# A four-layer graph network on one core: one setup program ahead of the first edge pass, and the node numbers worked out beside it

## The chip, the cores and the metric

The kernel runs on one NeuronCore of a Trainium2 chip. The metric is the device time of one execution in microseconds (us). Before the change it is 5416.98 us, the median of three runs (5415.43, 5416.98 and 5417.36).

## The reference

Inputs are x (3125 nodes of 256 features), 50,000 edges (`src`, `dst` sorted by `dst`, `edge_weight`) and the weights of four graph layers. Each layer's result is added to x and layer-normalised:

```python
x = _layernorm(x + _L0_gnn_ref(...))   # GCN: 3 layers of h = x @ fc.T + b; f = (h * deg_out**-0.5) @ ch_w;
                                       # segment_sum(f[src] * edge_w, dst) * deg_in**-0.5; relu; then one MLP
x = _layernorm(x + _L1_gnn_ref(...))   # edge conv: relu(theta(x_dst - x_src) + phi(x_src)), segment_max by dst
x = _layernorm(x + _L2_gnn_ref(...))   # graph attention with self loops, 8 heads, softmax by dst
x = _layernorm(x + _L3_gnn_ref(...))   # 3 edge-conv layers, segment_max by SRC, batch norm
```

`deg_out` and `deg_in` are the counts of edges per source and per destination. The fourth layer needs the edges in the order of `src`, so the kernel sorts them itself.

## The kernel before, in words

Edges are padded to 392 tiles (`ET`) of 128, handled as 98 groups (`NG`) of `GT` = 4 tiles; nodes fill 25 tiles (`NT`). The program is a row of stages, each a `Stage` with its own semaphores; every engine ends a stage before the next begins.

**Setup** is six stages, called at L1851 to L1856 and L1392. `constants` (L261) and `edge_columns` (L424) build identity and index rows and turn the edge lists into columns. `histogram` (L524) runs twice, for `dst` and for `src`: a node number is split into a high digit (98 values) and a low digit (32 values); for 14 tiles (`HB`) at a time VectorE makes both one-hots (L521), TensorE multiplies them per tile (L573), ScalarE keeps each tile's counts in `HIST` (L588); 28 such steps, then VectorE sums `HIST` over all tiles (L553) and sums up the start of each node's edges. Start and count go through DRAM (L599, L611) to become per-node columns. Beside the first histogram SyncE loads all weights (L309); beside the second TensorE turns the weights and multiplies the GCN's `GW` and `GB` (L379), and GpSimd scatters a flag to each node's first edge (`mark`, L650). `src_nodes` (L687) turns `HIST` into running positions with 32 scans (L703), works out the source numbers (`node_numbers`, L613) and the two degree factors. `n0` is a `node_products` stage (L887) that writes the first gather table, with the flags of the source nodes scattered beside it.

**An edge pass** (`edge_pass`, L1096) is a software pipeline over the 98 groups, on every engine in the order of its program. For group g: GpSimd gathers 4 x 128 rows of the table (L1146); ScalarE scales them by the edge weight (L1208, in the three GCN passes `e0` to `e2` alone); TensorE turns them into PSUM (`forth`, L1161); VectorE runs a segmented scan along the edges (`scan`, L1191, two instructions); TensorE turns the result back (`hither`, L1170); ScalarE moves it out (L1215); SyncE stores it and prefetches the indices, masks and weights of the group six further on (L1115 to L1132). In one step TensorE does `forth(g+1)` and then `hither(g)`; `hither(g)` waits for `scan(g)`.

Work "beside" a pass is added to that pipeline by `pipelined` (L84): a list of steps in front of the pass's own (early) and a list behind (late), each with a lead in groups. Two kinds matter here.

- `rank_beside` (L735), in `e0`, `e1` and `e2`: the rank of each edge within its source, for 4 tiles at a time (a rank step). Its parts, in the order in which they depend on each other: one-hots on VectorE (L762, L763), `flip` on TensorE (8 transposes, L787 and L788), `take` on ScalarE (L808 to L810), `meet` on TensorE (L796 to L798, 12 products), `places` on VectorE (L769 to L776). There are 98 rank steps, 33 in each pass (the last has 32), one for every third group. `meet` is an early step, in front of `forth` and `hither`; `places` is an early step of the group after it, in front of that group's `scan`.
- `order_beside` (L817), in `e3`: per group 12 `tensor_scalar` one-hots of full rows against one number per partition (L843 to L845).

Passes `e5` to `e7` have nothing beside them (the attention pass stands between `e3` and `e5`). `node_products` stages stand between the passes; `n4`, ahead of `e3`, uses no GpSimd.

Of the kernel before, what the change touches and what calls it, by code (L numbers as in the profile page):

```python
# [20 lines left out]
GT = 4  # L32
# [51 lines left out]
def pipelined(total, unroll, eng, *steps):  # L84

    most = max(lead for _, lead in steps)
    turns = (total - max(most, 3)) // unroll
# [8 lines left out]
    with eng.Fori(0, turns) as i:  # L98
        for j in range(unroll):
            for fn, lead in steps:  # L100
                fn(i * unroll + (j + lead), (j + lead) % unroll, i + (j + lead) // unroll)
    for s in range(turns * unroll, total):
        straight(s)
# [54 lines left out]
def build(nc, a, out):  # L158
    top = ExitStack()
    Stage.used = []  # L160
    with top:
# [7 lines left out]
        def carve(base, *wanted):  # L169
# [38 lines left out]
        HIST, key_hi, key_lo = carve(ARENA[:, NT * RW:NT * 3 * RW], ((ET, LO), F32), ((ET,), F32), ((ET,), F32))  # L208

        oh_hi, oh_lo, = carve(AGW_BASE, ((2, HB, HI), BF16), ((2, HB, LO), BF16))  # L210
        rank_hi, rank_lo, rank_t, rank_tf, rank_tmp, sel, rank = carve(
            AGW_BASE, ((2, RB, HI), BF16), ((2, RB, LO), BF16), ((2, 2, RB * P), BF16), ((2, RB * P), F32),
# [4 lines left out]
        key_tmp, iota_i, SRCF = carve(WORK, ((3, ET), I32), ((ET,), I32), ((ET,), F32))  # L217
# [12 lines left out]
        MW = sb("MW", [P, LAYERS, 2, D])  # L230
        TH1, DF1, W2 = sb("TH1", [P, 2, D]), sb("DF1", [P, 2, D]), sb("W2", [P, 2, D])
        WA = sb("WA", [P, 2, 2 * HEADS])
        TH3, DF3 = sb("TH3", [P, LAYERS, 2, D]), sb("DF3", [P, LAYERS, 2, D])
# [5 lines left out]
        pos = BYSRC[:, :].bitcast(F32)  # L239
        norm_out, norm_in = sb("norm_out", [P, NT]), sb("norm_in", [P, NT])  # L240
# [3 lines left out]
        MV = sb("MV", [P, NT, 2])  # L244
# [12 lines left out]
        flag_dst, flag_src = dram("flag_dst", [EP, 1]), dram("flag_src", [EP, 1])  # L257
        hist_start, hist_count = dram("hist_start", [2, NP]), dram("hist_count", [2, NP])


        def constants():  # L261
            with Stage(nc, "cst") as st:
                zeroed, filled, done = st.sem("zeroed"), st.sem("filled"), st.sem("done")
                copied = st.sem("copied")
                block = st.block()

                @block.gpsimd
                def _(eng):
                    eng.memset(ident[:, :], 0.0).then_inc(zeroed, 1)
                    eng.memset(ones[:, :], 1.0).then_inc(zeroed, 1)  # L270
                    eng.iota(iota_i[:, :], pattern=[[1, ET]], base=0, channel_multiplier=0).then_inc(zeroed, 1)
                    eng.wait_ge(zeroed, 3)
# [5 lines left out]
                    eng.affine_select(out=upto[:, :], in_=ones[:, :], compare_op=ALU.is_ge, fill=0.0,  # L278
                                      base=0, pattern=[[1, P]], channel_multiplier=-1).then_inc(filled, 1)

                @block.vector
                def _(eng):
                    eng.wait_ge(filled, 3)
                    eng.tensor_copy(identb[:, :], ident[:, :]).then_inc(copied, 1)
                    eng.tensor_copy(iota_b[:, :], iota_i[:, 0:P]).then_inc(copied, 1)
                    eng.tensor_copy(iota_h[:, :], iota_i[:, :]).then_inc(copied, 1)


        def weights_beside():


            fc, ch, mlp, th1, ph1, w2, fcb, fcb_wide, prod, AV = carve(
                WORK[:, 5 * ET:WORK.shape[1]], ((LAYERS * 2, D), F32), ((LAYERS * 2, D), F32), ((2, LAYERS * D), F32),
                ((2, D), F32), ((2, D), F32), ((2, D), F32), ((LAYERS * 2,), F32), ((LAYERS * 2, P), F32),
                ((2, 2, D), F32), ((2, D), F32))
            th3, ph3, B1b = carve(AGW_BASE[:, HB * (HI + LO):NT * RW], ((LAYERS * 2, D), F32), ((LAYERS * 2, D), F32), ((D,), F32))

            turns = [(lambda m, k, l=l: mlp[:, m, l * D + k * P:l * D + k * P + P], MW[:, l]) for l in range(LAYERS)]
            turns += [(lambda m, k: th1[:, m, k * P:k * P + P], TH1[:, :, :]),
                      (lambda m, k: ph1[:, m, k * P:k * P + P], DF1[:, :, :]),  # L300
# [54 lines left out]
            def turn_stage(st):  # L355
# [23 lines left out]
                def on_tensor(eng):  # L379
                    eng.wait_ge(weights_chain, 3 + 2 * LAYERS)  # L380
                    b = 0
                    for nat, _ in turns:
                        if b >= 4:
                            eng.wait_ge(weights_moved, b - 3)
# [1501 lines left out]
```

## Time and profile before

| what | us |
|---|---|
| median of three runs | 5416.98 |
| profiled execution, its span (first to last instruction) | 5421.3 |
| PE busy / DVE busy / ACT busy / POOL busy in it | 3436.3 / 3334.7 / 1890.6 / 3323.9 |
| setup, from 0 to the last tile of the first table | 283.0 |
| first gather of `e0`, `e1`, `e2`, `e3` at | 291.6, 876.1, 1458.8, 2096.8 |
| last gather of the same passes at | 784.2, 1367.8, 1951.3, 2590.6 |

The profile is of one execution, a different one from the three timed runs; its own time stands as its span, 4.3 us above the median. PE is TensorE, PEld its weight loads, DVE VectorE, ACT ScalarE, POOL GpSimd, SP SyncE. A busy share over the whole span mixes stages with different limits, so the rows further down are taken stage by stage.

### The profile page before, as it was taken

To read this page: it belongs to the slowest core of one execution; us is meant where nothing else is said; L and a number is where in the kernel's file an instruction comes from. 1 tells how busy PE (TensorE), PEld (TensorE's weight loads), DVE (VectorE), ACT (ScalarE), POOL (GpSimd) and SP (SyncE) were. 2 spreads that over 40 slices of the span, in tenths; PEclk is the share of its full clock that TensorE was granted. 3 is DMA by queue.
4 is the path that set the end of the run, shared out by engine and by line. 5 is a ranking of instruction groups with operands and counts; after the bars stand their busy time and mean duration, and the time that the engine had idled before them with its cause. 6 is when DMAs were issued, how large, how long until landed. Compare 5 with 4: busy or idle time off the path is not lost. (4 is left out here: it accounts for less than half of the span.)

```text
span 5421.3 us, 80197 instructions
## 1 busy us (share of the span) xinstructions
PE 3436.3 (63%) x18554; PEld 2760.3 (51%) x18554; DVE 3334.7 (62%) x6781; ACT 1890.6 (35%) x4275; POOL 3323.9 (61%) x3460
## 2 busy tenths in 40 slices
PE   3577777777787866666646664455556555665552
PEld 3456665666566655444534442355545555455451
DVE  8856655666566657999657775644444444444444
ACT  2256654666366643222223332222212222122221
POOL 1367765777477744777456664277752777357771
PEclk9778778788877778999666776777778777677776
DMA  3078875888488844888369995288853888358881
GB/s 89 16 197 235 235 210 151 239 234 234 128 236 234 235 136 137 234 233 234 110 170 241 248 242 152 65 230 236 237 163 103 236 237 236 96 169 235 236 230 52
DMA packets 965249, 1026.24 MB, mean 189 GB/s; under 512 B 312526, under 2 KB 843784, under 8 KB 965168
## 3 DMA queue, kind: packets, MB, share of 16 engines
q1 hardware_dynamic: 801184, 582.41, 36.8%
q0 software_dynamic: 163984, 442.92, 31.3%
q8 instruction: 30, 0.49, 0.0%
q14 instruction: 51, 0.42, 0.0%
HBM read 573.30 MB, written 449.41 MB: 189 GB/s over the span
## 5 line engine op out<-in xcount | busy, mean ns | idle before, releaser
L1146 POOL DMA_INDIRECT WORK<-table,idxbuf x2744 | 2609.6, 951 | 1319.6 <-issue 763.8
L1191 DVE TENSOR_TENSOR_SCAN WORK<-maskbuf,WORK,e_fm 128x512 f32<-128x512 bf16 x1372 | 1681.1, 1267 | 1293.7 <-PE e_fm L1161 1287.4
L1161 PE MATMUL e_fm<-ident,WORK 128*128 128x128 f32 x5488 | 997.2, 340 | 1044.1 <-DMA WORK<-table,idxbuf 717.5
L1161 PEld LDWEIGHTS e_fm<-ident,WORK 128*128 128x128 f32 x5488 | 790.1, 175 | 1218.8 <-DMA WORK<-table,idxbuf 725.2
L1215 ACT ACTIVATE WORK<-e_em 128x512 f32<-128x512 f32 x1372 | 757.1, 588 | 1607.6 <-PE e_em L1170 1491.3
L1170 PE MATMUL e_em<-ident,WORK 128*128 128x128 f32 x5488 | 995.2, 342 | 109.4 <-DVE WORK L1191 109.3
L1170 PEld LDWEIGHTS e_em<-ident,WORK 128*128 128x128 f32 x5488 | 884.6, 184 | 134.7 <-issue 112.4
L1208 ACT ACTIVATE WORK<-WORK,wbuf 128x256 f32<-128x256 f32 x1176 | 501.0, 496 | 605.2 <-DMA WORK<-table,idxbuf 605.2
L1545 POOL DMA_INDIRECT WORK<-table_attention,idxbuf x392 | 378.2, 965 | 189.5 <-issue 109.2
L1575 PE MATMUL att_o<-WORK 128*128 128x264 f32 x784 | 297.1, 543 | 0.0
L993 PE MATMUL n_t<-ident,WORK 128*128 128x128 f32 x450 | 108.9, 329 | 264.2 <-DVE WORK L966 156.3
L993 PEld LDWEIGHTS n_t<-ident,WORK 128*128 128x128 f32 x450 | 52.2, 156 | 339.0 <-DVE WORK L966 164.3
L1575 PEld LDWEIGHTS att_o<-WORK 128*128 128x128 f32 x784 | 199.5, 267 | 47.9
L521 DVE TENSOR_TENSOR ARENA<-ARENA,iota_b 128x128 bf16<-128x128 bf16 (+5 forms) x308 | 187.2, 665 | 1.4 <-DVEq L758 0.7
L1662 ACT ACTIVATE WORK<-att_o 128x264 f32<-128x264 f32 x392 | 151.1, 389 | 78.2 <-PE att_o L1575 73.4
L1559 PE MATMUL att_a<-ident,ARENA 128*32 128x128 f32 x98 | 33.4, 341 | 220.7 <-ACT ARENA L1649 220.1
L798 PE MATMUL e_ra<-ARENA 98*128 (+1 forms) x784 | 171.2, 302 | 0.0
L1329 PE MATMUL bn_ps<-ARENA,ones 128*128 128x256 f32 x300 | 105.0, 522 | 89.0 <-DVE ARENA L1355 79.0
L1559 PEld LDWEIGHTS att_a<-ident,ARENA 128*32 128x32 f32 x98 | 9.7, 99 | 274.9 <-ACT ARENA L1649 273.5
L798 PEld LDWEIGHTS e_ra<-ARENA 98*128 98x128 f32 x784 | 126.5, 203 | 28.8
L1329 PEld LDWEIGHTS bn_ps<-ARENA,ones 128*128 128x128 f32 x300 | 77.4, 266 | 116.6 <-DVE ARENA L1355 87.2
L844 DVE TENSOR_SCALAR ARENA<-iota_b,ARENA 128x128 bf16<-128x128 bf16 x392 | 133.3, 340 | 0.0
(282 smaller groups left out, 4519.9 us busy)
## 6 DMA issues: line engine op xcount, KB each, us to landing
edge_results<-WORK SPq DMA_DIRECT2D x686, 512.0 KB
edge_results_attention<-WORK SPq DMA_DIRECT2D x98, 544.0 KB
WORK<-table,idxbuf POOLq DMA_INDIRECT x2744
maskbuf<-nst_dst SPq DMA_DIRECT2D x294, 128.0 KB
maskbuf<-low_src SPq DMA_DIRECT2D x294, 128.0 KB, 4.9
ARENA<-dst_row SPq DMA_DIRECT2D x98, 256.0 KB
table<-ARENA SPq DMA_DIRECT2D x35, 640.0 KB, 3.2
maskbuf<-low_dst SPq DMA_DIRECT2D x98, 128.0 KB
```

Of the source, the lines that this page charges most:

```text
L521: return eng.tensor_tensor(dst, key[:, ds(t, n)].unsqueeze(2).broadcast_to([P, n, width]), iota_b[:, 0:width].unsqueeze(1).broadcast_to([P ...
L798: last = eng.matmul(pa[:, n * LO:(n + 1) * LO], rank_tf[0:HI, b, cols], HIST[0:HI, ds((k + first) * RB + n, 1), :].rearrange("p o l -> p ( ...
L993: last = eng.transpose(tp[slot][:, k * P:(k + 1) * P], R[:, slot, k * P:(k + 1) * P], ident[:, :])
L1146: eng.indirect_dma_start(G[:, q * GT + k, 0:D], None, T, bass.IndirectOffsetOnAxis(ap=idxbuf[:, q, k:k + 1], axis=0)).then_inc(got[q].sem, 16)
L1161: last = eng.transpose(fm[:, q % 2, h, k * P:(k + 1) * P], G[:, q * GT + k, h * P:(h + 1) * P], ident[:, :])
L1170: last = eng.transpose(em[:, pair, k, h * P:(h + 1) * P], S[:, q % 2, h, (2 * pair + k) * P:(2 * pair + k + 1) * P], ident[:, :])
L1191: last = eng.tensor_tensor_scan(S[:, q % 2, h, :], maskbuf[:, q, :], fm[:, q % 2, h, :], S[:, 1 - q % 2, h, GT * P - 1:GT * P], op0, op1)
L1208: last = eng.activation(G[:, q * GT + k, 0:D], G[:, q * GT + k, 0:D], ACT.Copy, scale=wbuf[:, q, k:k + 1])
L1215: eng.activation(O[:, q % 2, 2 * pair:2 * pair + 2, 0:D], em[:, pair], ACT.Copy).then_inc(pairs, 1)
L1329: last = eng.matmul(dst, ones[0:n, :], src[0:n, t, :], start=t == 0, stop=t == NT - 1)
L1545: eng.indirect_dma_start(G[:, q * GT + k, :], None, T2, bass.IndirectOffsetOnAxis(ap=idxbuf[:, q, k:k + 1], axis=0)).then_inc(got[q].sem, 16)
L1575: eng.matmul(po[:, k, 0:TW], same[:, q % 2, k, :], G[:, q * GT + k, :], start=True, stop=True).then_inc(made, 1)
```

## The change

- The six setup stages become one program, `setup()`. It counts the source nodes alone, and uses the counts for `norm_out` and the first table. Its one-hots come in pairs of tiles: keys, index row (`iota2`) and result are bf16, with the two tiles of a pair innermost. TensorE reads each tile of a pair with a step of two elements. GpSimd adds up each step's counts in place of VectorE's sum over `HIST`. Starts and counts become columns by a product with a selection matrix instead of a trip through DRAM. The masks by `dst` come from comparing each edge's `dst` with the one before it instead of a scatter. `GW` and `GB` are made between the two halves of the histogram. The first table's 25 tiles are made in the same program.
- Beside `e0`, now written out without a loop (`flat`), `numbers_and_weights_beside` does the rest: the histogram by `dst` in the first 49 groups (per group 16 `tensor_scalar` one-hots against one number per partition, and 8 accumulating products), the numbers of the source and destination nodes, the loads and turns of all weights not needed at first, and in 32 later groups one of the scans of `HIST` each.
- The 98 rank steps move from `e0` to `e2` into `e1` and `e2`: 49 in each, one for every second group, with three buffers. `meet` and `flip` are both late steps now, behind `hither`.
- The scatter of the source flags moves from `n0` to `n4`.

The core of the diff:

```diff
+        def one_hot_pairs(eng, dst, key, t, n, width):
+            shape = [P, n // 2, width, 2]
+            return eng.tensor_tensor(dst, key[:, ds(t, n)].rearrange("p (a b) -> p a b", b=2).unsqueeze(2).broadcast_to(shape),
+                                     iota2[:, 0:width, :].unsqueeze(1).broadcast_to(shape), ALU.is_equal)
...
+                    eng.memset(added[0:HI], 0.0).then_inc(summed, 1)
+                    with eng.Fori(0, steps) as i:
+                        eng.wait_ge(held, i + 3)
+                        eng.wait_ge(summed, i + 1)
+                        eng.tensor_tensor(added[0:HI], added[0:HI], HIST[0:HI, ds(i * HB, HB), :], ALU.add).then_inc(summed, 1)
...
+                                for k in range(HB):
+                                    last = eng.matmul(wide_ps[0:HI, b, k * LO:(k + 1) * LO], oh_hi[:, b, k // 2, :, k % 2],
+                                                      oh_lo[:, b, k // 2, :, k % 2], start=True, stop=True)
...
+                    hots(0, half // 2)
+                    eng.wait_ge(gcn_in, 14 * 16)
+                    for q in range(2 * LAYERS):
+                        eng.tensor_scalar(fcb_wide[:, q, :], ones[:, :], fcb[:, q:q + 1], None, ALU.mult).then_inc(wide, 1)
+                    hots(half // 2 * 2, (steps - half // 2 * 2) // 2)
...
+                    c.link(eng.tensor_reduce(count_src[:, :], added[0:HI].rearrange("p t l -> p l t"), AX.X, ALU.add))
...
+                        for k in range(DB):
+                            t = g * DB + k
+                            eng.tensor_scalar(dhi[:, g % 2, k, :], iota_b[:, 0:HI], dkey_hi[:, t:t + 1], None, ALU.is_equal)
+                            last = eng.tensor_scalar(dlo[:, g % 2, k, :], iota_b[:, 0:LO], dkey_lo[:, t:t + 1], None, ALU.is_equal)
+                        last.then_inc(dhot, 1)
...
-        RANKS = -(-(ET // RB) // LAYERS)
+        RANKS = ET // RB // 2
...
-                        if q % 3 == phase and not (isinstance(g, int) and g // 3 >= steps):
-                            fn(turn * (SETS // 3) + q // 3, q // 3 % 2)
+                        if q % 2 == phase and not (isinstance(g, int) and g // 2 >= steps):
+                            fn(turn * (SETS // 2) + q // 2, q // 2)
...
-                    return [(at(0, meet), 0)], [(at(0, flip), 2)]
+                    return [], [(at(0, meet), 0), (at(0, flip), 1)]
...
-                    return [(at(0, take), 1)], []
+                    return [(at(0, take), 0)], []
...
-            node_products("n0", stage_copy(X), GW[:, 0], out1, None, out2, table=(AGG, T), marks=(first_src, flag_src))
             for l in range(LAYERS):
-                edge_pass(f"e{l}", SRCI, (ALU.mult, ALU.add), nst_dst, True, rank_beside(l))
+                edge_pass(f"e{l}", SRCI, (ALU.mult, ALU.add), nst_dst, True, rank_beside(l) if l else numbers_and_weights_beside)
...
-            node_products("n4", None, DF1, copy_to(AGG), TH1, out2, table=(AGG, T), norm=(add_bias,))
+            node_products("n4", None, DF1, copy_to(AGG), TH1, out2, table=(AGG, T), norm=(add_bias,), marks=(first_src, flag_src))
...
-        constants()
-        edge_columns()
-        load_weights, turn_weights = weights_beside()
-        histogram(0, DSTF, load_weights)
-        histogram(1, SRCF, both_beside(turn_weights, dst_nodes_beside))
-        src_nodes()
+        setup()
```

## Rows read from the trace of the kernel before

**Rows 1.** The page, costliest groups: the gathers of the seven equal edge passes.

```profile
L1146 POOL DMA_INDIRECT WORK<-table,idxbuf x2744 | 2609.6, 951 | 1319.6 <-issue 763.8
```

**Rows 2.** Windows e1, e3, e5: length, busy PE, PEld, DVE, ACT, POOL, clock, DMA, GB/s.

```profile
876.00:1370.00 494.00, 378.83 (x2315) 316.57 (x2315) 308.90 (x610) 303.74 (x677) 373.45 (x392) 0.80 0.83 231
2097.00:2590.00 493.00, 340.35 (x2295) 241.67 (x2294) 483.59 (x1343) 103.49 (x190) 374.19 (x391) 0.97 0.82 230
3512.00:4001.00 489.00, 280.89 (x1543) 250.20 (x1544) 236.19 (x193) 109.81 (x191) 369.62 (x391) 0.73 0.83 233
```

**Rows 3.** Timeline of DVE in the setup: start, us, what.

```profile
20.13 15.82 DVE L521 TENSOR_TENSOR ARENA<-ARENA,iota_b 128x1372 bf16<-128x1372 bf16 x15 [0.35 <-DVE ARENA L512]
...
117.81 57.02 DVE L521 TENSOR_TENSOR ARENA<-ARENA,iota_b 128x1372 bf16<-128x1372 bf16 x56 [0.34 <-DVE ARENA L512]
177.03 21.69 DVE L553 TENSOR_REDUCE count<-ARENA 98x32 f32<-98x12544 f32 x1 [2.20 <-ACT ARENA L588]
...
209.12 29.73 DVE L703 TENSOR_TENSOR_SCAN ARENA<-ones,startv,ARENA 98x392 f32<-98x392 f32 x32 [5.21 <-PEq L155]
...
282.47 0.48 DVE L1086 SCALAR_TENSOR_TENSOR ARENA<-GB,norm_out,WORK 128x256 f32<-128x256 f32 x1 [0.38 <-ACT WORK L1081]
```

**Rows 4.** Timeline, second histogram: one TensorE step, and GpSimd's scatter beside it.

```profile
124.05 1.35 PE L573 MATMUL hist_ps<-ARENA 128*98 128x32 bf16 x14 [0.69 <-DVE ARENA L521]
124.61 1.73 POOL L650 DMA_INDIRECT flag_dst<-ones,first_dst  x1 [0.30 <-issue]
```

**Rows 5.** Timeline of POOL: a memset of the setup, and a scatter in n0.

```profile
4.51 0.52 POOL L445 MEMSET ARENA<- 98x512 f32 x1
...
244.11 0.97 POOL L650 DMA_INDIRECT flag_src<-ones,first_src  x1 [0.30 <-issue]
```

**Rows 6.** Groups by form, 16 to 210 us: the one-hots of high digits.

```profile
L521 DVE TENSOR_TENSOR ARENA<-ARENA,iota_b 128x1372 bf16<-128x1372 bf16 x56 | 88.6, 1583 | 0.7 <-DVE ARENA L512 0.7
```

**Rows 7.** Timeline of PE: the products of one tile in n0.

```profile
256.28 1.03 PE L1000 MATMUL n_m<-GW,WORK 128*128 128x256 f32 x4
```

**Rows 8.** Timeline of DVE: a scalar per partition, in the setup and in e3.

```profile
106.98 1.26 DVE L365 TENSOR_SCALAR WORK<-ones,WORK 128x128 f32<-128x128 f32 x6
...
2304.11 0.29 DVE L843 TENSOR_SCALAR ARENA<-iota_h,ARENA 128x392 bf16<-128x392 f16 x1
2304.33 0.40 DVE L844 TENSOR_SCALAR ARENA<-iota_b,ARENA 128x128 bf16<-128x128 bf16 x1
```

**Rows 9.** Timeline of e1, its start: meet's first product, forth, places, hither, scan.

```profile
887.68 0.31 PE L796 MATMUL e_rb<-ARENA 98*128 98x128 bf16 x1
...
891.25 1.95 PE L1161 MATMUL e_fm<-ident,WORK 128*128 128x128 f32 x8
891.47 0.29 DVE L769 SCALAR_TENSOR_TENSOR ARENA<-e_rb,upto 128x128 bf16<-128x128 f32 x1 [0.25 <-PE e_ra L798]
...
892.99 1.62 PE L1170 MATMUL e_em<-ident,WORK 128*128 128x128 f32 x8
...
893.42 4.94 DVE L1191 TENSOR_TENSOR_SCAN WORK<-maskbuf,WORK,e_fm 128x512 f32<-128x512 bf16 x4 [0.17 <-PE e_fm L1161]
```

**Rows 10.** The same, later: hither, flip's first and last, take's last, meet's first and last.

```profile
896.02 1.09 PE L1170 MATMUL e_em<-ident,WORK 128*128 128x128 f32 x8 [0.52 <-DVE WORK L1191]
...
896.95 0.22 PE L787 MATMUL e_ra<-identb,ARENA 128*98 128x128 bf16 x1
...
898.14 0.23 PE L788 MATMUL e_ra<-identb,ARENA 128*32 128x128 bf16 x1
...
901.35 0.57 ACT L810 ACTIVATE ARENA<-e_ra 98x512 f32<-98x512 bf16 x1
901.98 0.23 PE L796 MATMUL e_rb<-ARENA 98*128 98x128 bf16 x1 [0.42 <-ACT ARENA L810]
...
903.95 0.41 PE L798 MATMUL e_ra<-ARENA 98*128 x2
```

**Rows 11.** Window of n4, columns as in rows 2.

```profile
2016.00:2089.00 73.00, 55.69 (x250) 42.15 (x250) 53.39 (x200) 35.68 (x100) 0.00 (x0) 0.93 0.10 36
```

More of the change, by code:

```diff
@@ L97, in pipelined @@
         straight(s)
[L98 to L101, printed above, removed]
+    if turns:
+        with eng.Fori(0, turns) as i:
+            for j in range(unroll):
+                for fn, lead in steps:
+                    fn(i * unroll + (j + lead), (j + lead) % unroll, i + (j + lead) // unroll)
     for s in range(turns * unroll, total):
@@ new lines, in build, with one_hot @@
+        count_dst, start_dst, small = (v[0:HI] for v in carve(ROWSUMS, ((LO,), F32), ((LO,), F32), ((LO + 2,), F32)))
+        pick, rows_of = sb("pick", [HI, NT]), sb("rows_of", [HI, 4])
+        START, CNT, HAS, LASTE, T1, T2_ = range(6)
+        def one_hot(eng, dst, key, t, n, width):
+            return eng.tensor_tensor(dst, key[:, ds(t, n)].unsqueeze(2).broadcast_to([P, n, width]),
+                                     iota_b[:, 0:width].unsqueeze(1).broadcast_to([P, n, width]), ALU.is_equal)
@@ new lines, in split, with hots @@
+                    def split(key, hi, lo):
+                        c.inc(eng.tensor_scalar(key_tmp[:, 0], key, LO.bit_length() - 1, None, ALU.arith_shift_right))
+                        c.link(eng.tensor_scalar(key_tmp[:, 1], key, LO - 1, None, ALU.bitwise_and))
+                        c.inc(eng.tensor_copy(hi[:, :], key_tmp[:, 0]))
+                        c.link(eng.tensor_copy(lo[:, :], key_tmp[:, 1]))
+                    split(SRCI[:, :], key_hi, key_lo)
+                    def hots(first, turns):
+                        with eng.Fori(0, turns) as i:
+                            for b in range(2):
+                                n = i * 2 + (first + b)
+                                eng.wait_ge(made, n + 1)
+                                one_hot_pairs(eng, oh_hi[:, b], key_hi, n * HB, HB, HI).then_inc(hot_sem, 1)
+                                one_hot_pairs(eng, oh_lo[:, b], key_lo, n * HB, HB, LO).then_inc(hot_sem, 1)
@@ L602, in histogram @@
[L602 to L611 removed]
+                    eng.wait_ge(dst_in, 48)
@@ new lines, in _, with hold @@
+                    eng.activation(rows_f[:, 1], rows_i[:, 1], ACT.Copy).then_inc(cast_dst, 1)
+                    eng.sem_inc(held, 2)
+                    def hold(first, turns):
+                        with eng.Fori(0, turns) as i:
+                            for b in range(2):
+                                n = i * 2 + (first + b)
+                                eng.wait_ge(made, n + 3)
+                                eng.activation(HIST[0:HI, ds(n * HB, HB), :],
+                                               wide_ps[0:HI, b, 0:HB * LO].rearrange("p (k l) -> p k l", l=LO), ACT.Copy).then_inc(held, 1)
@@ L735, in rank_beside @@
+        RANKS = ET // RB // 2
         def rank_beside(layer):
-            first = layer * RANKS
-            steps = min(RANKS, ET // RB - first)
+            first = (layer - 1) * RANKS
+            steps = RANKS
             def beside(st, name):
```

813 lines of the change are left out of this document (425 added, 388 removed).

## The prediction

> **What bounds the kernel now.** I read the page first, then windows, then timelines, stage by stage. The page's largest group is GpSimd's gathers: 2744 of them, 951 ns each, with 764 us of "issue" between them, which is 1.23 us per gather [rows 1]; the table of times gives 491.7 us for the 391 gaps of `e1`, 1.26 each. Four make a group of edges, so GpSimd alone needs 5.0 us per group and 490 us per pass. The windows say the same of passes with very different work beside them: `e1` with rank steps 494 us, `e3` with 12 one-hots per group 493, `e5` with nothing 489 [rows 2]. So work beside a pass is free as long as it fits into 5.0 us per group. The reader should see how near the limit it already is: in `e3` VectorE is busy 484 of 493 us, in `e1` TensorE 379 of 494.
>
> The setup is bound otherwise, by one engine after another, VectorE above all: the first one-hots start at 20.1 us, 28 steps of the second histogram take 57.0, a sum over `HIST` 21.7, the scans of `HIST` 29.7, and the last tile of the first table is done at 283.0 [rows 3]. The profiled execution's span is 5421.3 us; the median of the runs is 4.3 below it. I apply differences to the median, 5417.
>
> **The setup, part by part.** (a) Up to the first one-hot: 20.1 us now [rows 3]. The new order needs `src` alone, and no stage ends in between; the remaining chain is load, cast, transpose, copy, split. I take 9. (b) 28 steps. One pair of one-hots costs 57.0/28 = 2.04 us now, 1.58 of it the high digits at one element per tick [rows 3, 6]. Packed in pairs the bound above is 2.04 (no gain), below 1.02 (half); I take 1.1. TensorE needs 1.35 per step [rows 4]; its operands get a step of two elements, which no row shows, and I leave it at 1.35 (above: twice). ScalarE is below that. New is GpSimd's addition, 448 elements with two reads and one write. The nearest row is a memset of 512 elements, one write, 0.52 us [rows 5]; one to three times that gives 0.46 to 1.4, and I take 1.05. Does it run beside the one-hots? In the second histogram GpSimd's scatters take 1.73 us and come every 2.03, exactly VectorE's step, while the same scatter in `n0` takes 0.97 [rows 4, 5]. They get one opening per step of VectorE's two-input one-hots. So I add up: 1.1 + 1.05 = 2.15 per step, 60 us; if they overlapped, TensorE would set 1.45 and 41 us.
>
> The Trainium skill's page "SBUF — State Buffer" (section "SBUF: two separate sides") says that a VectorE instruction with two SBUF inputs and a GpSimd one that reads SBUF exclude each other for their whole length. By that rule a step is the sum, by plain overlap TensorE's; the stretched scatters agree with the rule, though they don't show VectorE waiting.
>
> (c) Between the halves TensorE makes `GW` and `GB`: 12 products of 128x256 f32 per layer, 1.03 us per four [rows 7], so 9 us for three layers, plus 8 transposes. VectorE runs two steps ahead meanwhile; net 8. (d) The last step through TensorE, ScalarE and GpSimd, and a sum over 448 elements in place of 21.7 us [rows 3]: 4. (e) 25 tiles, each 1.03 of products and some 0.2 of transposes [rows 7]: 30 with filling the pipeline. Sum: 9 + 60 + 8 + 4 + 30 = 111, against 283.0. That is **-172**; with the overlap -190, with unpaired one-hots (2.04 + 1.05 per step) -146.
>
> What goes for nothing: the histogram by `dst`, its sum, the trips through DRAM and the weights' turns leave the path; what replaces the 32 scans lies in `e0`'s second half, about 1 us per group [rows 3] beside 2.45 of the pass's own scan. The scatter of flags moves to `n4`: 25 times 1.27 us is 32, and GpSimd is idle for all of `n4`'s 73 us [rows 11]. SyncE gets 3.4 MB of loads among `e0`'s stores; DMA is at 0.83 in a pass [rows 2] and gathers run groups ahead.
>
> **e0.** Rank steps go, 16 one-hots against a scalar come, per group for 49 groups. Price: six such in the setup stand 0.195 us apart (128 f32), one of 392 elements in `e3` 0.22 [rows 8]. These are 98 and 32 elements in bf16, shorter than both; below I let the length count and get 0.14, above 0.22. I take 0.17: 2.7 us, with 2.35 for the scan pair 5.05 per group, just at GpSimd's 5.0. The node numbers and weight steps add some 10 us of VectorE, most of which the groups in flight (up to six ahead) hide. **+5**; range -4 to +44 (0.22: 5.9 per group). The products wait for the one-hots (TensorE's late step) but `forth` of the next group is already done, so VectorE's order sets the pace, not the wait.
>
> **e1 and e2.** 49 rank steps per pass instead of 33 look harmless by busy time: TensorE's 379 us in `e1` [rows 2] would become some 440 of 494. But `meet` moves behind `hither`, and the chain closes in two groups instead of three. In order: `meet(k)`, at the end of TensorE's step g; `places(k)`, early in VectorE's step g+1 and so in front of `scan(g+1)`; `scan(g+1)`; `hither(g+1)`, which waits for it; `flip(k+1)` behind it; `forth`, `hither` of the next step; `meet(k+1)`. Nothing of it can overlap: each waits for the one before, by a semaphore or by its engine's order. Lengths: from `meet`'s end (`places` starts at 891.47) to `hither`'s start at 896.02, 4.55 us, places and scan [rows 9, 10]. Then at the high clock `hither` 0.93, `flip` 1.36, `forth` and `hither` 0.93 each (8 like products), `meet` 2.38 [rows 10]: 6.53. Together **11.1 us per two groups**, where GpSimd needs 10.0. `take` (three activations of 0.57) fits beside `forth` and `hither`. Before, the same chain had three groups, 15 us.
>
> At the low clock `forth` takes 1.74 and `meet` 3.79 [rows 9]; with `flip` stretched like `meet` the TensorE part is 11.2, the chain 15.7. Which clock will be granted? `e1` has 0.80 now, `e5` 0.73, `e3` with the densest TensorE work 0.97 [rows 2]; a share of 0.80 is 60% of the time at 2.4 GHz and 40% at 1.2. In the new chain TensorE stands idle for 4.55 - 0.93 = 3.6 us in every eleven, longer than any of its waits in the rows of `e1`, and works without a break otherwise. I take 0.83: the TensorE part is 7.6 (one over 0.66/6.53 + 0.34/11.2), the chain **12.2 us**. 49 of them are 598, against 492 from first to last gather: +106 per pass, **+212** for both. Bounds: 11.1 (+52 each) and 13 (+145 each).
>
> **Sum.** 5417 - 172 + 5 + 212 = 5462; I give 5460. The setup's gain pays for the two passes up to a chain of 11.8 us.
>
> **Rivals.**
> *Faster, the clock stays up.* The chain is there, but TensorE is at 0.9 or more in `e1` and `e2`, as in `e3`: 11.3 us, 554 per pass, +124. 5417 - 172 + 5 + 124 = 5374. For it: TensorE has more to do than in any pass but `e3`. Against: `e3`'s work is spread evenly, here it is one block and one hole. It decides below 11.8 us. Chance 0.30.
> *Much faster, no chain.* Something in the order lets `places` or `meet` slip beside other work, and a rank step costs the 0.1 us that it costs GpSimd now (494 against 489 for 33 of them [rows 2]): 5417 - 172 + 5 + 7 = 5257. Chance 0.08.
> *VectorE bounds e0.* At 0.22 per scalar one-hot: +44 instead of +5, 5500. For it: the 392-element form costs hardly more than the 128-element one, so length may not count at all. Chance 0.10.
> *The pairs don't pay.* The one-hots stay at one element per tick. The bf16 one-hots are at that rate now [rows 6]; no row that I read shows a packed one. Then +26: 5488. The Trainium skill's "VectorE: DVE Perf Modes" (section "The perf-mode tier table") gives `tensor_tensor` in bf16 twice the rate; its condition, steps of one in every operand, is what the pairs are for, and today's broadcast key breaks it, which the rows bear out. Chance 0.07.
> The forecast, within 5400 to 5520, has 0.45.
>
> A measurement of this kernel can tell about 0.2%, 11 us, from no change. From these cases: faster 0.39, within 0.2% 0.06, slower 0.55. The range takes in the clock's two ends with the setup's bounds, 5290 to 5560; the likeliest case alone spans 5400 to 5520.
>
> **What would show it.** First gather of `e0` near 120 us instead of 291.6. In `e1` and `e2` GpSimd's gathers no longer 1.25 apart but held by late prefetches; from one `meet` to the next 11 to 12.5 us; VectorE waiting for TensorE's `meet` ahead of `places`, and TensorE for the scan ahead of `hither`. `e0` at 490 to 500 us, `n4` unchanged. GpSimd's additions alternating with the one-hots, about 2.15 us per step. The forecast is wrong if `e1` stays at 5.0 us per group, or if the granted clock there is near 1.

## The result, and the profile after

The changed kernel takes **5613.0 us** (median of four runs, 5610.9 to 5615.7) against 5417.1 for the kernel before: a ratio of 1.0363, interval 1.0348 to 1.0377, so 3.6% slower. The forecast was 5460, its range 5290 to 5560: the side was right, the size was not, and the result lies 53 us outside the range. The profiled execution's span is 5609.2 us, 187.9 more than that of before. The first and last gathers of the passes say where it went:

| stretch, first gather to first gather | before | after | change | forecast |
|---|---|---|---|---|
| start to `e0` | 291.6 | 115.3 | -176.3 | -172 |
| `e0` to `e1` | 584.5 | 597.1 | +12.6 | +5 |
| `e1` to `e2` | 582.7 | 760.1 | +177.4 | +106 |
| `e2` to `e3` (with `n3`, `n4`) | 638.0 | 815.3 | +177.3 | +106 |
| `e3` to the end | 3324.5 | 3321.4 | -3.1 | 0 |

Two terms are off, and they are the same one twice. The page, costliest groups, shows it at a glance (columns: line engine operation out<-in xcount | busy us, mean ns | idle before us <-what ended most of it):

```profile
L1209 POOL DMA_INDIRECT WORK<-table,idxbuf x2744 | 2616.8, 954 | 1625.3 <-issue 763.3
L1233 PE MATMUL e_em<-ident,WORK 128*128 128x128 f32 x5488 | 1045.1, 354 | 395.5 <-DVE WORK L1254 391.3
L830 DVE SCALAR_TENSOR_TENSOR ARENA<-e_rb,upto 128x128 bf16<-128x128 f32 x392 | 90.5, 287 | 624.9 <-PE e_ra L859 624.9
```

The gathers are as long as before and their "issue" time is the same [rows 1]; their whole idle time has grown by 306 us, nearly all of it spent in something other than issue. `hither` (L1233) waits 391 us for the scan, and the first instruction of `places` (L830) waits 625 us for `meet` (L859): the two waits that the forecast named. Windows of `e1` and of `e3` (length, busy PE, PEld, DVE, ACT, POOL, granted clock, DMA share, GB/s), to be held against [rows 2]:

```profile
712.00:1365.00 653.00, 477.34 (x2636) 385.08 (x2637) 331.84 (x800) 325.76 (x711) 374.31 (x392) 0.74 0.62 173
2288.00:2782.00 494.00, 337.28 (x2297) 240.60 (x2296) 485.32 (x1343) 103.33 (x190) 374.89 (x392) 0.98 0.85 230
```

No engine in `e1` is busy for more than 73% of it, and the DMA share has fallen from 0.83 to 0.62: it is waits that set the pace. Here is one turn of the chain, timelines of TensorE and VectorE (start, us, engine line operation [idle before <-what ended it]):

```profile
909.35 0.41 PE L859 MATMUL e_ra<-ARENA 98*128 x2
909.59 1.07 PE L1224 MATMUL e_fm<-ident,WORK 128*128 128x128 f32 x8
914.21 1.97 PE L1233 MATMUL e_em<-ident,WORK 128*128 128x128 f32 x8 [3.54 <-DVE WORK L1254]
915.97 0.31 PE L848 MATMUL e_ra<-identb,ARENA 128*98 128x128 bf16 x1
...
917.91 1.97 PE L1224 MATMUL e_fm<-ident,WORK 128*128 128x128 f32 x8
919.67 1.53 PE L1233 MATMUL e_em<-ident,WORK 128*128 128x128 f32 x8
921.04 0.22 PE L857 MATMUL e_rb<-ARENA 98*128 98x128 bf16 x1
...
923.25 1.07 PE L1224 MATMUL e_fm<-ident,WORK 128*128 128x128 f32 x8
```

```profile
909.79 0.29 DVE L830 SCALAR_TENSOR_TENSOR ARENA<-e_rb,upto 128x128 bf16<-128x128 f32 x1 [6.37 <-PE e_ra L859]
...
911.62 2.45 DVE L1254 TENSOR_TENSOR_SCAN WORK<-maskbuf,WORK,e_fm 128x512 f32<-128x512 bf16 x2
...
923.45 0.29 DVE L830 SCALAR_TENSOR_TENSOR ARENA<-e_rb,upto 128x128 bf16<-128x128 f32 x1 [6.35 <-PE e_ra L859]
```

From `places` to `places` it is 13.66 us, one turn of the chain, and the turns of both passes all but repeat it (13.5 to 13.9). The parts, from start to start: `places` and scan 4.42 (909.79 to 914.21), `hither` 1.76, `flip` 1.94, `forth` 1.76, `hither` 1.37, `meet` with its way to VectorE 2.41. The TensorE part is 9.24 us; the forecast had 7.6. Look at where the long ones stand: `hither`, `flip` and `forth` behind the wait of 3.54 us take what they take at 1.2 GHz (1.97 for eight products, as [rows 9]), and by the time of `meet` the engine is back at 2.4 (0.22 for its first product; 0.23 in [rows 10]). The windows of this turn say the same: the wait, the TensorE part behind it, and the first 5.46 us of that part.

```profile
910.67:914.21 3.54, 0.00 (x0) 0.01 (x1) 3.30 (x8) 0.00 (x0) 2.63 (x4) 0.95 0.69 165
914.21:923.45 9.24, 9.24 (x50) 7.52 (x51) 2.89 (x5) 6.63 (x15) 4.20 (x5) 0.65 0.57 159
914.21:919.67 5.46, 5.46 (x25) 4.40 (x25) 2.88 (x4) 2.85 (x6) 3.99 (x5) 0.50 0.50 147
```

The columns are those of the windows above. The granted clock is still 0.95 while TensorE waits, 0.50 in the 5.46 us behind the wait, and 0.65 over the whole TensorE part (the medians over 89 turns of both passes are the same); the mean of the pass, 0.74, lies between.

The setup, timelines of VectorE, TensorE and GpSimd: the first pair of one-hots, twelve steps in the second half, the sum, the last tile of the first table; then one step of TensorE, and two of GpSimd's additions.

```profile
9.85 2.26 DVE L262 TENSOR_TENSOR WORK<-ARENA 128x1372 bf16<-128x1372 bf16 x4 [0.35 <-DVE ARENA L494]
...
47.80 22.51 DVE L262 TENSOR_TENSOR WORK<-ARENA 128x1372 bf16<-128x1372 bf16 x24 [7.80 <-PE set_wide L424]
...
73.76 0.90 DVE L517 TENSOR_REDUCE count_src<-WORK 98x32 f32<-98x448 f32 x1 [3.05 <-POOL WORK L341]
...
106.30 0.48 DVE L536 SCALAR_TENSOR_TENSOR ARENA<-GB,norm_out,WORK 128x256 f32<-128x256 f32 x1 [0.60 <-ACT WORK L588]
```

```profile
55.41 1.35 PE L424 MATMUL set_wide<-WORK 128*98 128x32 bf16 x14 [0.52 <-DVE WORK L262]
```

```profile
55.86 1.12 POOL L341 TENSOR_TENSOR WORK<-WORK,ARENA 98x448 f32<-98x448 f32 x1 [0.75 <-ACT ARENA L560]
...
72.67 0.98 POOL L341 TENSOR_TENSOR WORK<-WORK,ARENA 98x448 f32<-98x448 f32 x1 [0.89 <-ACT ARENA L560]
```

A step is 22.51/12 = 1.88 us. The first four one-hots, with no addition beside them yet, take 2.26, which is 1.13 for a step's pair (the forecast had 1.1); later VectorE counts as busy all the time and takes 1.88 for the same pair, and each addition starts 0.75 us after the one before it ends. An addition takes 1.12 us beside the one-hots and 0.98 once they are over.

### The profile page after: what moved, and what is told of

Same layout as the page of the kernel before. It is cut to its first block and busy times, and to the rows that moved or that the text cites. A ratio compares the mean times of both kernels' runs of the same rounds, so it can differ in the third digit from the quotient of the medians.

```text
span 5609.2 us, 78920 instructions
## 1 busy us (share of the span) xinstructions
PE 3510.0 (63%) x18564; PEld 2818.3 (50%) x18564; DVE 3331.3 (59%) x7488; ACT 1868.6 (33%) x4237; POOL 3324.5 (59%) x3471
## 5 line engine op out<-in xcount | busy, mean ns | idle before, releaser
L1224 PE MATMUL e_fm<-ident,WORK 128*128 128x128 f32 x5488 | 1024.1, 347 | 1020.6 <-DMA WORK<-table,idxbuf 793.3
L1224 PEld LDWEIGHTS e_fm<-ident,WORK 128*128 128x128 f32 x5488 | 821.6, 180 | 1180.0 <-DMA WORK<-table,idxbuf 775.1
L1233 PE MATMUL e_em<-ident,WORK 128*128 128x128 f32 x5488 | 1045.1, 354 | 395.5 <-DVE WORK L1254 391.3
L1233 PEld LDWEIGHTS e_em<-ident,WORK 128*128 128x128 f32 x5488 | 921.4, 191 | 443.3 <-issue 386.9
L830 DVE SCALAR_TENSOR_TENSOR ARENA<-e_rb,upto 128x128 bf16<-128x128 f32 x392 | 90.5, 287 | 624.9 <-PE e_ra L859 624.9
L1053 PE MATMUL n_t<-ident,WORK 128*128 128x128 f32 x400 | 96.3, 327 | 224.6 <-DVE WORK L1026 159.9
L1060 PE MATMUL n_m<-TURNED,WORK 128*128 128x256 f32 x600 | 177.0, 423 | 0.0
L859 PE MATMUL e_ra<-ARENA 98*128 (+1 forms) x784 | 161.0, 288 | 0.0
L1064 PE MATMUL n_m<-TURNED,WORK 128*128 128x256 f32 x600 | 159.2, 389 | 0.0
```

The lines of the kernel that those rows point to most:

```text
L859: last = eng.matmul(pa[:, n * LO:(n + 1) * LO], rank_tf[0:HI, b, cols], HIST[0:HI, ds((k + first) * RB + n, 1), :].rearrange("p o l -> p ( ...
L1060: last = eng.matmul(mps[:, slot, 0:D], XT[:, slot, k * P:(k + 1) * P], w1[:, k, :], start=k == 0, stop=k == 1)
L1064: last = eng.matmul(mps[:, slot, D:D + n2], XT[:, slot, k * P:(k + 1) * P], w2[:, k, :], start=k == 0, stop=k == 1)
L1224: last = eng.transpose(fm[:, q % 2, h, k * P:(k + 1) * P], G[:, q * GT + k, h * P:(h + 1) * P], ident[:, :])
L1233: last = eng.transpose(em[:, pair, k, h * P:(h + 1) * P], S[:, q % 2, h, (2 * pair + k) * P:(2 * pair + k + 1) * P], ident[:, :])
```

## The experiments

Each run stands against runs of the kernel before on the same chip. Edits are to the changed kernel unless said otherwise.

### places behind the scan

```diff
-                    return [(at(1, places), 0)], [(at(0, one_hots), 3)]
+                    return [], [(at(1, places), 0), (at(0, one_hots), 3)]
```

> The changed kernel with one step moved: VectorE does places behind the scan of its group instead of in front of it, same operations, same counts. Theory of the closed chain (meet, places, scan, hither, flip, forth, hither, meet: 13.66 us per two groups in e1 and e2 of the changed kernel): scan and hither leave the chain, what stays is meet 2.4, places 1.8, flip 1.4 to 1.9, forth and hither 1.9 to 3.5, which is 7.5 to 9.6 and below GpSimd's 10.0. e1 and e2 go back to 492 to 500 us from first to last gather, about 170 us less each with the tail: 5260 to 5285 in all. Rival, 49 rank steps per pass are too much work (TensorE at the clock it is granted, or VectorE): order is no cure, e1 and e2 stay above 600 us, the total above 5500.

5254.6 us (5252.7 to 5260.1), ratio to before 0.971, interval 0.9694 to 0.9726. One step moved past another on one engine is worth 358 us. The window of `e1`, and a turn on TensorE and VectorE:

```profile
713.00:1205.00 492.00, 426.44 (x2677) 345.97 (x2677) 342.83 (x803) 325.30 (x721) 372.43 (x392) 0.83 0.83 231
```

```profile
952.08 1.09 PE L1233 MATMUL e_em<-ident,WORK 128*128 128x128 f32 x8 [0.91 <-DVE WORK L1254]
...
955.64 0.29 DVE L830 SCALAR_TENSOR_TENSOR ARENA<-e_rb,upto 128x128 bf16<-128x128 f32 x1 [1.21 <-PE e_ra L859]
```

`e1` is at 491.4 us with all its 49 rank steps, GpSimd is the bound again, and `hither` waits 0.91 us in place of 3.54. So neither the count of rank steps nor their cost on any engine was at fault. All that differed was that `scan` stood behind `places`, and through it `hither` behind `meet`.

### The hole filled with needless work

```diff
                     def hither(g, q, turn):
+                        if name in ("e1", "e2") and q % 2 == 1:
+                            eng.wait_ge(pairs, g * 2 + 3)
+                            for k in range(24):
+                                eng.transpose(em[:, 0, k % 2, k // 2 % 2 * P:(k // 2 % 2 + 1) * P], ident[:, :], ident[:, :])
                         eng.wait_ge(scanned, g + 3)
```

> The changed kernel with 24 needless TensorE products (128x128 f32, target e_em, overwritten afterwards) ahead of hither's wait in every second group of e1 and e2, where TensorE stands idle for 3.5 us: more work, the same chain. Theory that the hole is what keeps the clock down in the first six us of each block: 24 at 0.116 us are 2.8 us and fit in the hole, hither, flip and forth run at the high rate, the period falls from 13.66 to 4.4 + 3 x 0.93 + 1.36 + 2.4 = 11.0 us, 130 us less per pass, 5350 in all, though TensorE does more. Rival, the clock is low for another reason (too much work, or the level of the chip): the 24 take 5.3 us, 1.8 more than the hole, the period is 15.5 and the total 5790.

5339.8 us (5334.1 to 5345.5), ratio 0.9864, interval 0.9844 to 0.9884: 273 us less than the changed kernel, by adding 2352 products to it.

```profile
715.00:1241.00 526.00, 477.89 (x3776) 406.34 (x3776) 333.59 (x801) 322.62 (x713) 372.34 (x391) 0.98 0.77 215
```

```profile
911.03 2.78 PE L1231 MATMUL e_em<-ident 128*128 128x128 f32 x24
914.66 1.09 PE L1237 MATMUL e_em<-ident,WORK 128*128 128x128 f32 x8 [0.84 <-DVE WORK L1258]
915.59 0.22 PE L848 MATMUL e_ra<-identb,ARENA 128*98 128x128 bf16 x1
...
916.94 1.09 PE L1224 MATMUL e_fm<-ident,WORK 128*128 128x128 f32 x8
```

The clock is at 0.98, `hither` takes 0.93 to the next start where it took 1.76, and the turn is 10.82 us (median of 96). That is the forecast's length at the high clock, 11.1, to within 0.3; the chain was laid out rightly, and the clock was the whole of the error. The Trainium skill's page "TensorE: Matmul & The Clock Gate" (section "HAM oscillation — how this bites in real kernels") describes the like for a loop that waits for a transfer in every turn: each burst of products starts at half clock again. The traces agree: with a wait of 3.54 us in each turn `hither`, `flip` and `forth` run at the low clock, with one of 0.84 none of them does.

### places made longer, take made longer

```diff
-                        eng.wait_ge(passed, k * 6 + 5)
-                        eng.tensor_reduce(rank[:, 1, :], sel[:, :, :], AX.X, ALU.add).then_inc(passed, 1)
-                        eng.wait_ge(passed, k * 6 + 6)
+                        for n in range(4):
+                            eng.wait_ge(passed, k * 9 + (n + 5))
+                            eng.tensor_reduce(rank[:, 1, :], sel[:, :, :], AX.X, ALU.add).then_inc(passed, 1)
+                        eng.wait_ge(passed, k * 9 + 9)
```

> The changed kernel with three more reductions of 128x128 in places, each behind the one before: about 0.37 us each, 1.1 us in all. Chain theory: places lies on the chain, so each of the 98 periods grows by 1.1 us: +110 us, 5720 in all, although VectorE is busy for half of e1 and e2 alone. Rival, something else sets the pace (TensorE's work, GpSimd, a transfer): within 15 us of 5613.

5771.3 us (5767.2 to 5775.4): +158, where 110 was expected; three reductions are 0.96 us, and 98 of those 94.

```profile
712.00:1441.00 729.00, 530.48 (x2632) 421.94 (x2632) 369.22 (x937) 328.37 (x711) 373.73 (x391) 0.61 0.54 155
```

```profile
915.79 0.41 PE L860 MATMUL e_ra<-ARENA 98*128 x2
916.03 1.07 PE L1225 MATMUL e_fm<-ident,WORK 128*128 128x128 f32 x8
921.62 1.97 PE L1234 MATMUL e_em<-ident,WORK 128*128 128x128 f32 x8 [4.52 <-DVE WORK L1255]
...
929.25 0.64 PE L860 MATMUL e_ra<-ARENA 98*128 x2
```

The turn goes from 13.66 to 15.36 us on average (turns of 14.4 and 16.3 alternate). 0.96 of the 1.70 is the work; the rest is that the hole has grown (4.5 us in one turn, 3.7 in the next) and that the low clock lasts longer behind it, in the second turn shown into `meet` (0.64 for two of its products, 0.41 in the turn before). The clock of the pass is 0.61.

For `take` the same was tried with two more activations in front of its three (each waiting for the one before it).

> The changed kernel with two more activations of 98x512 in take, each behind the one before: 1.2 to 1.3 us more on ScalarE in each of 98 rank steps. Chain theory: take ends 1.5 us ahead of meet, beside forth and hither, so it is off the chain: within 15 us of 5613. Rival, any engine's extra work shows because all are coupled: +120 us.

5612.3 us (5609.7 to 5614.9), a turn of 13.66 us: nothing, for 98 times 1.15 us of ScalarE (382.0 us busy in `e1`, where it was 325.8). Together the two runs draw the chain: a microsecond on it costs more than itself, one beside it costs nothing.

### meet back in front

```diff
-                    return [], [(at(0, meet), 0), (at(0, flip), 1)]
+                    return [(at(0, meet), 0)], [(at(0, flip), 1)]
```

> The same kernel as before under this edit, since that run's chip moved about 160 GB/s in the passes in place of 235 and made them wait for transfers. Theory of the chain in two groups: meet 2.4, scan and places 4.4, hither 0.93, flip 1.4, take 1.9: 11.0 at the high clock, up to 13 at the low one; e1 and e2 take 540 to 640 us, the total is 5330 to 5560. Rival, the late meet alone is to blame: 492 to 500 us each and 5255.

5400.0 us (5391.1 to 5404.1), ratio 0.9957, interval 0.9943 to 0.9972; `e1` takes 556.5 us, a turn 11.35 (median). So the late `meet` alone isn't it: put back, the chain closes through `take` (`meet` waits 1.64 us for ScalarE) and is still above the 10 us of two groups.

```profile
916.56 0.23 PE L857 MATMUL e_rb<-ARENA 98*128 98x128 bf16 x1 [1.64 <-ACT ARENA L871]
...
919.31 1.95 PE L1224 MATMUL e_fm<-ident,WORK 128*128 128x128 f32 x8
```

The low clock is here too (0.77 in `e1`): the longest wait of this turn is 1.64 us, and `forth` behind `meet` takes 1.95. So a wait of 3.5 us is not the only thing that brings it.

### The kernel before, with meet late

```diff
-                    return [(at(0, meet), 0)], [(at(0, flip), 2)]
+                    return [], [(at(0, meet), 0), (at(0, flip), 2)]
```

> The same kernel as before under this edit, for the same reason. Chain theory: 13.7 us is below the 15 that three groups give, so nothing changes: within 10 us of the kernel before. Rival, a late meet costs 3.66 us per rank step: +350 us.

5543.4 us (5541.9 to 5545.0), ratio 1.0224, interval 1.0205 to 1.0243. Both expectations missed. I had carried the 13.66 over; but with three groups to a rank step the order of TensorE's program runs through one more `forth` and `hither`, and the wait ahead of `hither` is there as well:

```profile
959.37 1.96 PE L1170 MATMUL e_em<-ident,WORK 128*128 128x128 f32 x8 [3.54 <-DVE WORK L1191]
961.12 0.31 PE L787 MATMUL e_ra<-identb,ARENA 128*98 128x128 bf16 x1
```

A turn is 16.3 us, above the 15.0 of three groups. At the high clock it should be 12.7 (10.8 and the 1.9 of one more `forth` and `hither`). That was then tried, with the same 24 products in every third group of the three passes:

> The same kernel as before under this edit, whose run was on a chip with slower transfers (7.3 us per group whatever the order). Theory: 12.9 us at the high clock, below the 15 of three groups, so the passes go back to 492 to 496 us and the total to 5415 to 5430, though work is added. Rival: 5540 and more.

5432.8 us (5422.4 to 5440.7), ratio 1.0022, interval 1.0010 to 1.0033; the turn is 15.0, GpSimd's, and `e1` has 493.4 us at a clock of 0.93. So in this kernel, too, it is the clock that makes the chain bind. That it is 12.7 us at the high clock is not shown: the run says only that it is below the 15.0 of three groups.

### The setup: unpaired one-hots, and no addition on GpSimd

The first edit puts `one_hot` in the place of `one_hot_pairs` and lets TensorE read contiguously. The second:

```diff
-                    with eng.Fori(0, steps) as i:
...
-                        eng.tensor_tensor(added[0:HI], added[0:HI], HIST[0:HI, ds(i * HB, HB), :], ALU.add).then_inc(summed, 1)
...
-                    c.link(eng.tensor_reduce(count_src[:, :], added[0:HI].rearrange("p t l -> p l t"), AX.X, ALU.add))
+                    c.link(eng.tensor_reduce(count_src[:, :], HIST[0:HI].rearrange("p t l -> p l t"), AX.X, ALU.add))
```

> The changed kernel with plain one-hots in the setup in place of those in pairs, TensorE reading them contiguously. Theory that VectorE's one-hots and GpSimd's addition take turns: a step is now 1.87 us (about 0.9 and 0.97); with the one-hots at 2.04 as before the change it is 3.0, 28 steps are 32 us more, the last tile comes at 139 in place of 107, the total is 5645. Rival, they overlap: a step is 2.04, +5 us.

> The changed kernel with GpSimd's 28 additions taken out; VectorE sums all of the 392 counts at once at the end, as before the change. Theory of turns: without the additions a step falls from 1.87 to TensorE's 1.35 to 1.45, 12 to 14 us less over 28 steps, and the sum costs 21.7 in place of some 2: the last tile comes about 6 us later. Rival, the pair of packed one-hots needs 1.87 by itself: steps stay at 1.87 and the last tile comes 19 us later.

Both fell on a chip whose transfers were slower (below), so their whole times can't be held against 5613; but the setup's steps wait for no transfer, and its timeline up to the first table can. VectorE unpaired, then VectorE without the addition:

```profile
61.30 33.89 DVE L256 TENSOR_TENSOR WORK<-ARENA,iota_b 128x1372 bf16<-128x1372 bf16 x24 [7.53 <-PE set_wide L424]
...
131.13 0.48 DVE L536 SCALAR_TENSOR_TENSOR ARENA<-GB,norm_out,WORK 128x256 f32<-128x256 f32 x1 [0.60 <-ACT WORK L588]
```

```profile
15.33 2.34 DVE L262 TENSOR_TENSOR WORK<-ARENA 128x1372 bf16<-128x1372 bf16 x4 [0.39 <-PE set_wide L420]
...
59.99 21.06 DVE L513 TENSOR_REDUCE count_src<-ARENA 98x32 f32<-98x12544 f32 x1 [1.82 <-ACT ARENA L556]
...
112.46 0.48 DVE L532 SCALAR_TENSOR_TENSOR ARENA<-GB,norm_out,WORK 128x256 f32<-128x256 f32 x1 [0.60 <-ACT WORK L584]
```

Unpaired, a step is 33.89/12 = 2.82, and the last tile comes 24.8 us later (131.1 against 106.3; expected 32). Without the addition a step is 1.37, TensorE's, and VectorE now waits for TensorE; the last tile comes 6.2 us later for the long sum (expected 6). So the addition costs 0.5 us per step that nothing hides, and VectorE pays for it: a pair of packed one-hots goes from 1.13 to 1.88 us, an unpaired one from 2.04 [rows 3] to 2.82, by 0.75 and 0.78. That is less than an addition's 0.98, so some 0.2 us of each do run side by side. The additions save more than they cost, the pairing saves 25 us.

### e0: what makes it 14 us longer

`e0`'s gathers take 506.3 us from first to last, 492.6 before. Read group by group, groups 7 to 10 take 27.0 us in place of 20, and from group 57 on it is 212.2 in place of 205.1.

For the first part I moved the numbers of the source nodes from groups 1, 3 and 5 to 36, 38 and 40, alone and with `places` behind the scan.

> The changed kernel with the numbers of the source nodes moved from groups 1, 3 and 5 of e0 to 36, 38 and 40 and nothing else. Theory: groups 7 to 10 of e0 lose their 7 us, e1 and e2 stay at 652 us: 5606 in all. Rival, the loads: e0 stays at 506 us.

> The changed kernel with places behind the scan and, in e0, the numbers of the source nodes (three steps of some 10 us of VectorE together) moved from groups 1, 3 and 5 to 36, 38 and 40. Theory for e0's start, where groups 7 to 10 take 27.0 us in place of 20.0: VectorE falls behind in the first groups by those steps, and GpSimd meets it once it is six groups ahead; later VectorE has its lead back, and the 7 us go: e0's gathers take 500 in place of 507 us, the total is 5247. Rival, the weights' loads beside the first stores and gathers make the delay: e0 and the total (5254) stay.

Alone: 5613.1 us in its one run, `e0` 512.1, groups 7 to 10 29.9. With the other edit: 5262.2 (5245.1 to 5269.1), ratio 0.9707, interval 0.9694 to 0.9720, which is that of `places` behind the scan by itself; `e0` 504.9, groups 7 to 10 25.7. In the five other traces of the changed kernel's `e0` on chips with fast transfers, it is 507 to 512 us and groups 7 to 10 take 28 to 29; so most of the 7 us are still there and the theory of VectorE's 10 us fell. What the timelines of the changed kernel show there are ScalarE waiting for SyncE (the store two groups back) and GpSimd for its indices:

```profile
161.70 1.09 ACT L1278 ACTIVATE WORK<-e_em 128x512 f32<-128x512 f32 x2 [2.43 <-SPq L1189]
```

```profile
164.78 0.94 POOL L1209 DMA_INDIRECT WORK<-table,idxbuf  x1 [3.63 <-DMA wbuf<-WE]
```

The loads of weights stand in SyncE's queue at that place. An edit spreads them, one for every third group, with the turns of the weights from group 24 on:

> The changed kernel with places behind the scan, and in e0 the eight loads of weights one for every third group (groups 1 to 22) in place of two or three each in groups 1, 2 and 3; the turns start at group 24 in place of 8. Theory that these loads, in front of the first prefetches in SyncE's queue and beside the first stores, make groups 7 to 10 of e0 take 7 us too long: e0's gathers take 501 in place of 508 us, the total is 5247. Rival, it is the start of the pass itself (its first scans and waits): 507 us and 5254.

Both of its runs fell on chips with slower transfers (6924 and 6815 us, the kernel before 7122 and 7068), where its `e0` as a whole can't be told from others. Group by group there is a hint: with the loads spread, groups 7 and 8 take 5.3 to 5.5 and 5.0 us, with the loads where the change puts them 6.1 to 7.2 and 6.8 to 7.8 (five runs on such chips). But group 9 then takes 14 in place of 7 to 9. That the loads cost the 7 us is argued, not shown.

The second part is better shown. The 32 scans over `HIST` were put into `e0`'s last group (with `places` behind the scan):

```diff
-                    if groups + 9 <= g < groups + 9 + LO:
-                        lo = g - (groups + 9)
+                    for lo in range(LO) if g == NG - 1 else ():
```

> The same kernel as before under this edit, for the same reason. Theory of scans that hold up gathers: e0's first to last gather 500 in place of 508, the total 5278. Rival: 508 and 5286.

The total is of a chip with slower transfers again (6822 us, the kernel before 7068 on it); the length of a gather on GpSimd hangs on them little (median 0.946 us on both kinds of chip). With the scans in groups 58 to 89, gathers of groups 58 to 92 last 8.4 us more in all than 0.946 each (20 of the 140 are longer than 1.02); with them at the end it is nothing, with not one above 1.02, in both runs of this edit. The two runs with the loads spread, on the same two chips and with the scans where they were, have 20 and 21 long ones. In the changed kernel all 20 long gathers start under such a scan and end 0.8 us behind it; a gather that has started before the scan does keeps its 0.95:

```profile
431.88 1.01 DVE L745 TENSOR_TENSOR_SCAN ARENA<-ones,start_src,ARENA 98x392 f32<-98x392 f32 x1
```

```profile
431.99 1.71 POOL L1209 DMA_INDIRECT WORK<-table,idxbuf  x1 [0.30 <-issue]
```

That `e0` itself gets shorter by that much no run on a chip with fast transfers shows.

## Why the prediction was wrong, point by point

**The setup, -172: right** (-176.3; last tile at 107 where I had 111), and by its own steps nearly: first one-hot at 9.85 (9), packed pair 1.13 (1.1), 25 tiles at 1.08 (1.2). The addition takes 0.98 (1.05) by itself but adds only 0.75 to a pair, so a step is 1.88 and not 2.15. Some luck is in the sum: the 28 steps came to 51 us for my 60, the stretch between the halves to 10 for 8, and from the last one-hot to the last tile it was 36.5 for 34. The turn-taking that I took from the stretched scatters [rows 4] is shown by the two runs on it, with VectorE waiting too, which [rows 4] could not show. The rule of the Trainium skill's page "SBUF — State Buffer" (section "SBUF: two separate sides"), that the two instructions exclude each other for their whole length, is borne out nearly: 1.13 and 0.98 would be 2.11, and a step is 1.88. The pairs pay (2.04 to 1.13); that rival is out.

**e0, +5: +12.6, inside its range.** The price of a scalar one-hot was 0.149 us (201.58 to 203.96 for sixteen), below my 0.17, so VectorE had 4.83 us per group and was no bound; that rival is out as well. What I had put down as costing nothing cost 7 to 8 us: the scans of `HIST` "lie in `e0`'s second half, about 1 us per group". I counted VectorE's time there and forgot that I had just used the shared port in the setup. The other 7 us stand where the loads are, which I had also put at nothing; their cause stays open.

**n4: right.** From `n3`'s first gather to `e3`'s it is 128.5 us (128.2 before); the scatter of flags costs nothing.

**e1 and e2, +212: +354.7. This is the step that failed, and within it one number: the clock.** The chain was the right one, in its order and in its 4.4 and 6.5 us; filling the hole gives 10.82 where the forecast's high end is 11.1. I took the mean clock that a pass would be granted (0.83) and spread it evenly over the TensorE part, 7.6 us. It was 9.24. The formula was good: with the 0.65 that the TensorE part was granted it gives 9.2, with the 0.74 of the whole pass 8.3, a chain of 12.9. So about half of the 1.6 us missing is that the mean itself came out below my 0.83, and half that I spread a mean evenly. A mean over a pass counts idle time too, and low and high phases don't fall evenly: the wait itself is nearly all at the high clock (0.95) and the low one stands behind it, which is just the part of the work that everyone waits for. I took [rows 9] for "the low clock" and weighed them by a mean, instead of asking what TensorE had done before them: they are the pass's first products. A stretch of `e1` of the kernel before that I had not read says it plainly (timeline of TensorE):

```profile
1181.29 1.97 PE L1161 MATMUL e_fm<-ident,WORK 128*128 128x128 f32 x8 [3.01 <-ACT WORK L1208]
1183.05 1.66 PE L1170 MATMUL e_em<-ident,WORK 128*128 128x128 f32 x8
...
1186.51 1.09 PE L1161 MATMUL e_fm<-ident,WORK 128*128 128x128 f32 x8 [0.55 <-ACT WORK L1208]
```

Behind 3.01 us of idleness eight products take 1.97, five us later 1.09; and I had worked out a hole of 3.6 us for every turn of the new chain. With 13.66 my own sum gives, 49 turns against the 492 from first to last gather, +177 per pass: 5417 - 172 + 5 + 354 = 5604, 9 us from the result. (From first to last gather `e1` grew by 160.5 only; the rest of its 177 comes behind the last gather, since GpSimd runs groups ahead.) The bound of 13 was too low for the same reason. A chain of 13.66 was in reach of the two ends that I had, 11.1 and 15.7.

**The rivals.** "The clock stays up" (0.30, 5374) is what the run with the filled hole is: 5340. "No chain" (0.08, 5257) is the kernel with `places` behind the scan: 5255. They were sound as mechanisms; what chose between the first and the result was the wait of 3.5 us.

## What to carry to other kernels

When work beside a loop is moved, follow the wait through every engine's program order until it comes back to where it began, count in how many groups it closes, and compare that with what the loop gives, at both clocks of TensorE; busy shares don't show it. Price TensorE's work behind such a wait (3.0 to 4.5 us in these traces) at the low clock and never by a stage's mean, since a hole lengthens the chain that made it. And put a step that waits for a far result behind the step that others wait for, not in front: here that is worth 358 us, and gives the best version of all, 5254.6 us, 2.9% faster than the kernel before.

## What the hardware showed that I had not expected

- More work made it faster: 2352 needless products took 273 us off, by keeping TensorE at 2.4 GHz behind a wait (clock of the pass 0.98 in place of 0.74).
- A microsecond on the chain cost 1.8 (1.70 for 0.96), since it lengthened the low clock's share as well.
- A VectorE scan with both inputs in SBUF holds up the indirect transfers that GpSimd issues: 1.71 us for one that starts 0.11 after the scan does, 0.95 otherwise. The pass's own scans, of 1.24 us each and with one input in PSUM, don't. The Trainium skill's page "SBUF — State Buffer" (section "SBUF: two separate sides") tells of such a stall behind copies in a two-port mode; here it is a plain f32 scan.
- Chips differ. Nine runs (of every edit here but `places` and `take` longer, `places` behind the scan alone, the filled hole in the changed kernel, and the moved numbers) fell on chips on which this program's passes moved 140 to 180 GB/s in place of 230, and took 7.0 to 8.1 us per group in `e1`; the kernel before took 7068 to 7122 us. `meet` back in front gave 6857 there (interval 0.954 to 0.986), the kernel before with `meet` late 6969 (0.969 to 1.003). With the hole filled as well it was 7271 (1.014 to 1.030), slower than the kernel before, and no run tells why. The changed kernel itself was not run there, but the two setup variants, which hold its chain whole, were 3.4% and 3.7% *faster* than the kernel before (intervals 0.951 to 0.981 and 0.950 to 0.976). The chain costs little there: its 13.7 us fit into two groups of 7.3, and `e1` takes 711 and 725 us with it, 727 to 737 in the four runs with `places` behind the scan on two other such chips. Window of `e1` and of `e3` in the unpaired one:

```profile
938.00:1662.00 724.00, 526.41 (x2632) 418.70 (x2632) 327.42 (x784) 327.43 (x711) 371.00 (x391) 0.63 0.57 156
2717.00:3440.00 723.00, 387.07 (x2255) 285.63 (x2256) 481.73 (x1314) 105.61 (x186) 371.40 (x391) 0.78 0.54 155
```

The pass with the chain and the one without it take the same here (711 and 693 us in the other setup variant). What slows the transfers there no run tells.
